# A fourth slot for attention features, and the second batch's statistics, gates and rotations moved ahead of the first scores

## Chip, cores and metric

The kernel runs on one core of one Trainium2 chip. The metric is the time of one execution on the device in microseconds (us), the median of several runs.

## The reference, cut to what matters

```python
x = L0_attn_x                                  # (8, 512, 128) fp32, 8 batches of 512 tokens
mod = (silu(c) @ wmod).reshape(8, 6, 1, 128)   # sa, ca, ga, sb, cb, gb; ga, gb kept at least 0.25 in size
h = layernorm(x) * (1 + ca) + sa
q, k, v = split(h @ qkv_w.T + qkv_b)           # 16 heads of 8
q, k = rope(q), rope(k)
attn = softmax(causal(q @ k.T / sqrt(8)))      # (8, 16, 512, 512)
x = x + ga * ((attn @ v) @ proj_w.T + proj_b)
h = layernorm(x) * (1 + cb) + sb
y = square(relu(h @ W_fc.T)) @ W_proj.T
x = x + gb * spikes(y) / 5                     # how often in 5 steps an integrator passes its threshold: 0 to 5
```

## The kernel before, in words

The work is cut into **halves**: half n is 8 of the 16 heads of batch n // 2, so there are 16 halves. Each engine runs a list of instructions in its own order, written out by hand, and the lists meet at semaphores. There is no scheduler.

Of each half the scores are made twice. First `scores_for_max` (L548, L554) makes them with queries in rows, in 21 banks called k, and VectorE takes the negated maximum of each row (`maxima`, L978). GpSimd splits the maxima in two bf16 parts, TensorE transposes them (L565 for the first half, L578), ScalarE copies them out (`mrow`, L833 and L841), and SyncE writes them by DMA into two extra rows of the query features `qf` (L429, L434), so that the second product subtracts them. Then `scores_for_exp` (L593, L598) makes the transposed scores in 18 banks called u, ScalarE takes exponentials (L827), and `probs_times_v` (L611) multiplies them with the values. The main loop counts slots u, 18 a half and 36 a batch; `at` is the slot within the batch. Maxima run ahead by up to 31 banks (`scores_ahead`): half 2b+2 is needed at about slot 9 of batch b, half 2b+3 at about slot 27.

The features of a head are its rotated queries and keys in three bf16 parts each (`parts` 0, 1, 2). After `rotary` on VectorE (L1014, `rot_c` and `rot_s`), the sum `whole` and what is left after a part (`rest`, L1299, and part 2, L1303) come from GpSimd, parts 0 and 1 from ScalarE (L885). SyncE stores every part to DRAM (`store_part`, L396) and reads them back spread over partitions: `spread_queries` (L409, 576 KB) and `spread_keys` (L420, three DMAs of 192 KB). They land in slot n % RING of `qf` and `kf`. `spread_queries(n)` waits until the slot's last user, half n - RING, has made its last transposed scores (`t_ready`). All DMAs are issued by SyncE, in its order.

Around this lie, one batch ahead, the layer norm (`statistics1`, `normalise1`, GpSimd's `deviation1`), its transposition (`a_task` T1), the products for queries (QK), keys (QK + 1) and values (V_); and one batch behind, the outputs' moves (`move_outputs`, L440 and L444), reciprocals of the sums (`reciprocals`, L1020, L448, L453), the normalised outputs `o_n` (L1325), and on TensorE the projection (PROJ, slot 16), then T2, FC and Y_ of the feed-forward part (`D_AT`, `Y_AT`), all in `d_bank`.

Ahead of the loop, TensorE does both batches' first tasks, mixed with `keep_warm`: products of a table with the identity that nobody reads. One call with SEQ columns is the same shape as a query or key task. Then come 22 banks of the first scores, each with a filler of 160 columns.

```python
def spread_queries(n, own=slice(0, HH), done=None):
    ...
    reach(sp, t_ready, NU * (n - RING + 1))
```

## Time and profile before

| | us |
|---|---|
| median of 3 runs | 441.04 |
| lowest and highest run | 440.73, 445.44 |
| the profiled execution's own time | 443.15 |
| its span in the trace | 441.4 |
| TensorE's matmuls busy | 390.9 (89% of the span) |
| VectorE busy | 329.3 (75%) |
| ScalarE busy | 256.8 (58%) |
| GpSimd busy | 126.1 (29%) |

The span is the time between the first and the last instruction of the trace. The execution's own time has 1.75 us around it. That execution was 2.1 us above the median. A busy engine is not the same as a bound: where an engine is waited for is read from the waits.

### The profile page before, as it was taken

To read this page: it belongs to the slowest core of one execution; us is meant where nothing else is said; L and a number is where in the kernel's file an instruction comes from. 1 tells how busy PE (TensorE), PEld (TensorE's weight loads), DVE (VectorE), ACT (ScalarE), POOL (GpSimd) and SP (SyncE) were. 2 spreads that over 40 slices of the span, in tenths; PEclk is the share of its full clock that TensorE was granted. 3 is DMA by queue.
4 is the path that set the end of the run, shared out by engine and by line. 5 is a ranking of instruction groups with operands and counts; after the bars stand their busy time and mean duration, and the time that the engine had idled before them with its cause. 6 is when DMAs were issued, how large, how long until landed. Compare 5 with 4: busy or idle time off the path is not lost.

```text
span 441.4 us, 15622 instructions
## 1 busy us (share of the span) xinstructions
PE 390.9 (89%) x6599; PEld 253.1 (57%) x6599; DVE 329.3 (75%) x730; ACT 256.8 (58%) x447; POOL 126.1 (29%) x163
## 2 busy tenths in 40 slices
PE   2778899888999989998899999998998889988885
PEld 2327555555656755666457654765566646753653
DVE  6659995886886988878986997699866777541176
ACT  8203465565676756765666665766665457566523
POOL 6714310430343043503342234304330220040020
PEclk9989999999999999999999999999999899998999
DMA  7056363243314233242415251323233050011001
GB/s 214 22 161 169 99 218 88 70 116 102 104 45 119 75 101 93 80 122 49 137 50 139 64 138 48 117 72 99 67 113 86 16 146 6 25 45 27 3 1 49
DMA packets 26050, 38.53 MB, mean 87 GB/s; under 512 B 5796, under 2 KB 20716, under 8 KB 23692
## 3 DMA queue, kind: packets, MB, share of 16 engines
q1 hardware_dynamic: 25980, 37.53, 29.8%
q8 instruction: 52, 0.85, 0.8%
q14 instruction: 18, 0.15, 0.1%
HBM read 26.35 MB, written 8.65 MB: 79 GB/s over the span
## 4 chain that ended last, share of the span: by engine, by line
PE 41%; DMA 18%; DVE 13%; ACT 10%; POOL 6%; issue 5%; SPq 5%; ACTq 0%; POOLq 0%; DVEq 0%
PE o_bank L611 10%; DMA kf<-k_scr 9%; PE d_bank L528 7%; DVE negmax L978 6%; PE t_bank L593 6%; PE s_bank L548 5%; DMA rden<-r_scr 4%; ACT probs L827 4%; PE a_bank L528 3%; DMA r_scr<-rden_c 2%; POOL parts L1303 2%; PE s_bank L528 2%; SPq L440 2%; PE t_bank L528 2%; POOL o_n L1325 2%
## 5 line engine op out<-in xcount | busy, mean ns | idle before, releaser
L978 DVE TENSOR_REDUCE negmax<-s_bank 128x1 f32<-128x512 f32 (+7 forms) x368 | 192.9, 566 | 56.9 <-PE s_bank L554 54.6
L827 ACT ACTIVATE probs<-t_bank 128x512 f32<-128x512 f32 x288 | 163.0, 594 | 89.8 <-PE t_bank L598 84.5
L548 PE MATMUL s_bank<-kf,qf 126*64 126x512 bf16 (+7 forms) x1024 | 118.7, 293 | 11.8 <-DMA kf<-k_scr 6.2
L593 PE MATMUL t_bank<-qf,kf 128*64 128x512 bf16 (+7 forms) x1024 | 113.3, 290 | 10.8 <-ACT probs L827 9.8
L611 PE MATMUL o_bank<-probs,v 128*32 128x512 f32 (+7 forms) x1024 | 75.1, 412 | 0.0
L548 PEld LDWEIGHTS s_bank<-kf,qf 126*64 126x64 bf16 x1024 | 50.6, 111 | 40.6 <-DVE negmax L978 19.9
L554 PE MATMUL s_bank<-causal,identb 128*64 128x64 bf16 x1024 | 72.6, 195 | 0.0
L598 PE MATMUL t_bank<-causal_t,identb 128*64 128x64 bf16 x1024 | 64.8, 195 | 0.0
L593 PEld LDWEIGHTS t_bank<-qf,kf 128*64 128x64 bf16 x1024 | 41.4, 110 | 35.1 <-ACT probs L827 14.4
L598 PEld LDWEIGHTS t_bank<-causal_t,identb 128*64 128x64 bf16 x1024 | 48.1, 111 | 9.3 <-issue 0.2
L554 PEld LDWEIGHTS s_bank<-causal,identb 128*64 128x64 bf16 x1024 | 47.1, 112 | 8.3 <-issue 8.1
L611 PEld LDWEIGHTS o_bank<-probs,v 128*32 128x32 f32 x1024 | 26.8, 109 | 36.3 <-issue 23.4
L1293 POOL TENSOR_TENSOR whole<-rot_c,rot_s 128x512 f32<-128x512 f32 x15 | 19.1, 1274 | 53.9 <-DVE rot_s L1014 53.9
L528 PE MATMUL d_bank<-wpr_sb,sq 128*64 128x128 f32 x448 | 30.1, 276 | 0.0
L1271 POOL CAST mparts<-negmax 128x32 bf16<-128x32 f32 x15 | 3.2, 211 | 94.2 <-DVE negmax L978 94.2
L528 PEld LDWEIGHTS d_bank<-wpr_sb,sq 128*64 128x64 f32 x448 | 24.0, 137 | 4.2 <-issue 3.0
L1303 POOL TENSOR_TENSOR parts<-rest,parts 128x512 bf16<-128x512 f32 x15 | 17.5, 1169 | 30.0 <-ACT parts L885 30.0
L528 PE MATMUL d_bank<-h2T,wfc_sb 128*64 128x512 f32 x96 | 25.5, 609 | 0.0
L1325 POOL TENSOR_TENSOR o_n<-o_t,rden 128x512 f32<-128x512 f32 x7 | 9.5, 1360 | 47.6 <-DMA rden<-r_scr 47.6
L1014 DVE SCALAR_TENSOR_TENSOR rot_c<-a_bank,bqk_sb,cos_sb 128x512 f32<-128x512 f32 x14 | 10.5, 750 | 16.3 <-PE a_bank L528 15.7
L528 PE MATMUL t_bank<-cos_sb,ident 128*64 128x160 f32 (+2 forms) x152 | 22.6, 404 | 0.0
L885 ACT CAST parts<-whole 128x512 bf16<-128x512 f32 x15 | 9.3, 618 | 22.4 <-POOL whole L1293 22.3
(145 smaller groups left out, 455.9 us busy)
## 6 DMA issues: line engine op xcount, KB each, us to landing
qf<-q_scr SPq DMA_DIRECT2D x15, 576.0 KB
kf<-k_scr SPq DMA_DIRECT2D x45, 192.0 KB
q_scr<-parts SPq DMA_DIRECT2D x24, 128.0 KB, 1.7
k_scr<-parts SPq DMA_DIRECT2D x24, 128.0 KB, 1.7
xa<-in_x SPq DMA_DIRECT2D x8, 256.0 KB, 3.9
o_t<-o_raw SPq DMA_DIRECT2D x60, 32.0 KB, 2.4
rden<-r_scr SPq DMA_DIRECT2D x15, 128.0 KB
out_y<-count SPq DMA_DIRECT2D x7, 256.0 KB, 6.7
```

The costliest lines, as they stand in the source:

```text
L528: last = nc.tensor.matmul(bank[own, cols], weights[:, own], data, start=start, stop=stop)
L548: nc.tensor.matmul(bank[C * a:C * (a + 1), col:col + keys], qf[0:KS, slot, 2 * p + a, C * i:C * (i + 1)], kf[0:KS, slot, 2 * p + a, 0:keys ...
L554: last = nc.tensor.matmul(bank[C * a:C * (a + 1), end - C:end], identb[:, C * a:C * (a + 1)], causal[:, C * a:C * (a + 1)], start=False, s ...
L593: nc.tensor.matmul(bank[C * a:C * (a + 1), col:col + w], kf[0:KX, slot, 2 * p + a, C * kb:C * (kb + 1)], qf[0:KX, slot, 2 * p + a, C * kb: ...
L598: last = nc.tensor.matmul(bank[C * a:C * (a + 1), col:col + C], identb[:, C * a:C * (a + 1)], causal_t[:, C * a:C * (a + 1)], start=False, ...
L611: last = nc.tensor.matmul(o_bank[32 * p:32 * (p + 1), C * kb:SEQ], v32[:, b % 2, NP * kb + HP * half + p, :], probs[:, v, col:col + w], st ...
L827: nc.scalar.activation(probs[:, v, :], t_bank[u % 2][:, :], ACT.Exp, scale=SCALE).then_inc(e_done, 1)
L978: last = nc.vector.tensor_reduce(own[:, i, p:p + len(same)], cols, AX.X, ALU.max, negate=True)
L1014: nc.vector.scalar_tensor_tensor(dst[to, qk, :], bank[of, :], bqk_sb[of, qk:qk + 1], table[of, :], ALU.add, ALU.mult).then_inc(rotated if ...
L1293: nc.gpsimd.tensor_tensor(whole[:, qk, :], rot_c[:, qk, :], rot_s[:, qk, :], ALU.add)\
L1303: nc.gpsimd.tensor_tensor(parts[:, qk, 2, :], rest[:, qk, :], parts[:, qk, 1, :], ALU.subtract).then_inc(split_done, 1)
L1325: nc.gpsimd.tensor_tensor(o_n[:, :], o_t[:, :], rden[:, :], ALU.mult).then_inc(on_done, 1)
```

## The change

It does six things.

- `RING` goes from 3 to 4 slots of features. The memory comes from sharing: `rest` is `rot_s`, `sq` is `relu` (squares are made in place), the modulation weights lie in `relu`, the row of ones in `count`. `rotary` waits for the last batch's split where it writes `rot_s`.
- SyncE issues the queries of half 2b+4 at the end of batch b, one store ahead of its keys' last part; the keys keep their place.
- The projection goes from slot 16 to 17, the residual from 18 to 19, the second reciprocals from slot 10 to 9.
- VectorE does the second batch's statistics, the gates' sizes and the normalisation ahead of the first rotation, and both rotations of the second batch ahead of the first maxima.
- TensorE does the second batch's values ahead of the first scores, and two long fillers there in place of four ahead of the second batch's transposition.
- ScalarE clears the fourth slot between steps of the start. GpSimd writes the ones beside the values by partition halves, with no `affine_select`. All parts of the second batch are stored ahead of the first maxima's rows.

```diff
--- before.py
+++ after.py
@@ -34,7 +34,7 @@
 NP = H // 2
-RING = 3
+RING = 4
 HALF = SEQ // 2
@@ -87,7 +87,7 @@
 
-D_AT = {16: PROJ, 25: T2, 27: FC, 29: FC + 1, 31: FC + 2, 33: FC + 3}
+D_AT = {17: PROJ, 25: T2, 27: FC, 29: FC + 1, 31: FC + 2, 33: FC + 3}
 Y_AT = {36: 0, 37: 1, 38: 2, 39: 3}
@@ -179,14 +179,12 @@
         ct_sb = sb("ct_sb", [P, NB])
-        wmod_sb = sb("wmod_sb", [P, 6 * P])
         cos_sb = sb("cos_sb", [P, SEQ])
...
         causal_t = sb("causal_t", [P, P], BF16)
-        ones_row = sb("ones_row", [MR, SEQ], BF16)
         minus_half = sb("minus_half", [P, NT])
@@ -210,7 +208,8 @@
         whole = sb("whole", [P, 2, SEQ])
-        rest = sb("rest", [P, 2, SEQ])
+
+        rest = rot_s
         parts = sb("parts", [P, 2, NPART, SEQ], BF16)
@@ -239,8 +238,13 @@
         relu = sb("relu", [P, NF, SEQ])
-        sq = sb("sq", [P, NF, SEQ])
+
+        sq = relu
+
+        wmod_sb = relu[:, 0:2, :].rearrange("p i c -> p (i c)")[:, 0:6 * P]
         count = sb("count", [P, 2, SEQ])
+
+        ones_row = count[0:MR, 0, 0:SEQ // 2].bitcast(BF16)
 
@@ -464,26 +468,24 @@
             sp.wait_ge(ones_made, 1)
-            sp.wait_ge(zeros_made[2], 2)
+            for slot in (2, 3):
+                sp.wait_ge(zeros_made[slot], 2)
             sp.dma_start(kf[KS:KX].rearrange("r s h c -> r (s h) c"),
...
             sp.dma_start(g_scr, gate_t[:, :]).then_inc(gates_stored, 16)
-            for j in range(NPART):
-                store_part(1, 0, j)
+            for qk in range(2):
+                for j in range(NPART):
+                    store_part(1, qk, j)
             place_first_maxima(0)
-            spread_queries(2)
-            for j in range(NPART):
-                store_part(1, 1, j)
-            spread_keys(2)
+            spread(2)
             place_first_maxima(1)
...
                     store_part(b + 1, 1, 2)
-                if 0 < b < final:
-                    spread(2 * b + 2)
+                    spread_keys(2 * b + 2)
                 if b == 0:
@@ -511,6 +513,7 @@
                     store_part(b + 2, 1, 1)
+                    spread_queries(2 * b + 4)
             spread_reciprocals(final, 0)
@@ -711,17 +714,16 @@
             pe.wait_ge(rotary_loaded, 16 * 2)
-            keep_warm(t_bank[1], SEQ, 4)
             a_task(1, T1)
...
             a_task(1, QK + 1)
+            a_task(1, V_)
+            keep_warm(t_bank[1], SEQ, 2)
             for k in range(NS_FIRST + 3):
...
                 keep_warm(t_bank[1], 160)
-                if k == 5:
-                    a_task(1, V_)
             transpose_first_maxima(0)
@@ -850,7 +852,7 @@
                 if b == 0:
-                    act.wait_ge(v_placed_ones, 1)
+                    act.wait_ge(v_placed_ones, 2)
                 for a in range(2):
@@ -898,18 +900,20 @@
             modulate1(0)
-            for j in range(2):
-                take_part(0, 0, j)
+            take_part(0, 0, 0)
             place_values(0)
+            take_part(0, 0, 1)
             modulate1(1)
+            clear(3, qf)
             act.wait_ge(d_ready, SETUP_TASKS)
             nc.scalar.copy(gate_t[:, :], d_bank[0:3 * NB, 0:P]).then_inc(gates_out, 1)
+            clear(3, kf)
             take_part(1, 0, 0)
...
             take_part(1, 0, 1)
-            first_maxima_out(0)
             for j in range(2):
                 take_part(1, 1, j)
+            first_maxima_out(0)
 
@@ -1007,7 +1011,7 @@
                 dve.wait_ge(a_ready, 4 * b + QK + qk + 1)
-                reach(dve, whole_done, 2 * (b - 1) + qk + 1)
+                reach(dve, whole_done if step == 0 else split_done, 2 * (b - 1) + qk + 1)
                 to, of, dst, table = ((slice(0, P), slice(0, P), rot_c, cos_sb),
@@ -1074,7 +1078,7 @@
 
-            def gates():
+            def gate_sizes():
                 for n, j in enumerate((2, 5)):
@@ -1087,6 +1091,8 @@
                 last.then_inc(mod_step, 1)
+
+            def gates():
                 dve.wait_ge(d_ready, 2)
@@ -1124,6 +1130,10 @@
             normalise1(0)
+
+            statistics1(1)
+            gate_sizes()
+            normalise1(1)
             dve.wait_ge(wqk_loaded, 16 * 2)
@@ -1131,16 +1141,12 @@
             first_k_parts()
-            statistics1(1)
-            normalise1(1)
             gates()
...
                 rotary(1, 0, step)
-            for k in range(NS_FIRST):
-                maxima(k)
             for step in range(3):
                 rotary(1, 1, step, bank=d_bank)
-            for k in range(NS_FIRST, scores_ahead(-1)):
+            for k in range(scores_ahead(-1)):
                 maxima(k)
@@ -1161,9 +1167,9 @@
                 if b > 0:
-                    if at == (8 if b == final else 10):
+                    if at == (8 if b == final else 9):
                         reciprocals(b - 1, 1)
-                    if at == 18:
+                    if at == (18 if b == final else 19):
                         residual1(b - 1)
@@ -1348,22 +1354,20 @@
             for a in range(2):
-                ones = v32[:, :, :, 16 + HD * a:16 + HD * (a + 1)].rearrange("p k g d -> p (k g) d")
-                nc.gpsimd.memset(ones, 1.0).then_inc(v_cleared, 1)
-                pool.wait_ge(v_cleared, 2 + a)
-                last = nc.gpsimd.affine_select(out=ones, in_=ones, pattern=[[0, 2 * NC * NP], [0, HD]], fill=0.0,
-                                               compare_op=ALU.is_ge, base=(C - 1, -C)[a],
-                                               channel_multiplier=(-1, 1)[a])
-            last.then_inc(v_placed_ones, 1)
+                ones = v32[C * a:C * (a + 1), :, :, 16 + HD * a:16 + HD * (a + 1)].rearrange("p k g d -> p (k g) d")
+                nc.gpsimd.memset(ones, 1.0).then_inc(v_placed_ones, 1)
+
+                pool.wait_ge(v_placed_ones, a + 1)
+            deviation1(1)
             rotary_sum(0, 0)
...
             left(0, 0, 2)
-            deviation1(1)
             for qk in range(2):
...
                 left(1, qk, 2)
-                split_first_maxima(qk)
+            for pairs in range(2):
+                split_first_maxima(pairs)
 
```

VectorE near the program's start, around the first batch's rotations (`st`, `mv` are statistics, `xn` the normalised input, `sign` and `big` the gates' sizes). Before:
```order
L994 TENSOR_SCALAR xn<-xa,mv,rs 128x128 x4
L1014 SCALAR_TENSOR_TENSOR rot_c<-a_bank,bqk_sb,cos_sb 128x512
L1014 SCALAR_TENSOR_TENSOR rot_s<-a_bank,bqk_sb,sin_sb 64x512 x2
L1014 SCALAR_TENSOR_TENSOR rot_c<-d_bank,bqk_sb,cos_sb 128x512
L1014 SCALAR_TENSOR_TENSOR rot_s<-d_bank,bqk_sb,sin_sb 64x512 x2
L1101 TENSOR_TENSOR whole<-rot_c,rot_s 128x512
L1105 CAST parts<-whole 128x512
L1108 TENSOR_TENSOR rest<-whole,parts 128x512
L1112 CAST parts<-rest 128x512
L1115 TENSOR_TENSOR parts<-rest,parts 128x512
L983 BN_STATS st<-xa 128x6 x4
L989 BN_AGGR mv<-st 128x2 x4
```
In the change:
```order
L1079 TENSOR_SCALAR mod<-mod 128x8 x2
L998 TENSOR_SCALAR xn<-xa,mv,rs 128x128 x4
L987 BN_STATS st<-xa 128x6 x4
L993 BN_AGGR mv<-st 128x2 x4
L1083 TENSOR_SCALAR sign<-mod 128x8
L1084 SCALAR_TENSOR_TENSOR big<-mod 128x8
L1083 TENSOR_SCALAR sign<-mod 128x8
L1084 SCALAR_TENSOR_TENSOR big<-mod 128x8
L1088 TENSOR_SCALAR big<-big 128x16
L1091 SCALAR_TENSOR_TENSOR gate<-sign,big 128x8 x2
L998 TENSOR_SCALAR xn<-xa,mv,rs 128x128 x4
L1018 SCALAR_TENSOR_TENSOR rot_c<-a_bank,bqk_sb,cos_sb 128x512
```
The second batch's statistics, gate sizes and normalisation, which stood behind the first key parts, now stand ahead of the first rotation.

SyncE at the end of batch 0 and the start of batch 1 (`kf`, `qf` are the features' slots, `k_scr` the keys' parts in DRAM). Before:
```order
L396 DMA k_scr<-parts 128x512
L434 DMA qf<-mrow 2x4x1024
L448 DMA r_scr<-rden_c 64x64
L396 DMA k_scr<-parts 128x512 x2
L409 DMA qf<-q_scr 72x1x4096
L420 DMA kf<-k_scr 24x1x4096 x3
L453 DMA rden<-r_scr 64x1x512
```
In the change:
```order
L400 DMA k_scr<-parts 128x512
L438 DMA qf<-mrow 2x4x1024
L452 DMA r_scr<-rden_c 64x64
L400 DMA k_scr<-parts 128x512
L413 DMA qf<-q_scr 72x1x4096
L400 DMA k_scr<-parts 128x512
L424 DMA kf<-k_scr 24x1x4096 x3
L457 DMA rden<-r_scr 64x1x512
```
The queries' load went ahead of the last store of a key part; the keys' loads stayed behind it.

TensorE around the projection of batch 0, in batch 1 (`wo_g`, `o_n`: gated projection weights and normalised outputs). Before:
```order
L593 MATMUL t_bank<-qf,kf 64x256 x4
L598 MATMUL t_bank<-causal_t,identb 64x64 x4
L528 MATMUL d_bank<-wo_g,o_n 64x128 x8
L548 MATMUL s_bank<-kf,qf 64x192 x4
L548 MATMUL s_bank<-kf,qf 64x64 x4
L554 MATMUL s_bank<-causal,identb 64x64 x8
L593 MATMUL t_bank<-qf,kf 64x256 x4
L598 MATMUL t_bank<-causal_t,identb 64x64 x4
L548 MATMUL s_bank<-kf,qf 64x128 x8
```
In the change:
```order
L596 MATMUL t_bank<-qf,kf 64x256 x4
L601 MATMUL t_bank<-causal_t,identb 64x64 x4
L551 MATMUL s_bank<-kf,qf 64x192 x4
L551 MATMUL s_bank<-kf,qf 64x64 x4
L557 MATMUL s_bank<-causal,identb 64x64 x8
L596 MATMUL t_bank<-qf,kf 64x256 x4
L601 MATMUL t_bank<-causal_t,identb 64x64 x4
L531 MATMUL d_bank<-wo_g,o_n 64x128 x8
L551 MATMUL s_bank<-kf,qf 64x128 x8
```
One slot's scores (192 and 64 columns of one kind, 256 of the other) went ahead of the projection.

## Rows read from the trace of the kernel before

**Rows 1.** Busy time by stretch: PE, PEld, DVE, ACT, POOL; granted clock, DMA share, GB/s.
```profile
45.00:58.00 13.00, 10.96 (x210) 7.45 (x208) 12.97 (x35) 5.41 (x10) 3.96 (x6) 1.00 0.44 123
...
123.00:170.00 47.00, 44.57 (x814) 29.33 (x810) 39.48 (x88) 30.52 (x55) 14.73 (x18) 1.00 0.34 94
```
**Rows 2.** What TensorE's matmuls waited for: total us, times, longest.
```profile
PE t_bank L593 <- ACT probs L827: 9.8, 21, 1.2
PE s_bank L548 <- DMA kf<-k_scr: 6.2, 6, 1.4
...
PE d_bank L528 <- POOL o_n L1325: 5.7, 5, 1.5
```
**Rows 3.** Timeline of VectorE's start: start us, us, instruction, idle before it.
```profile
14.69 0.75 DVE L1014 SCALAR_TENSOR_TENSOR rot_c<-a_bank,bqk_sb,cos_sb 128x512 f32<-128x512 f32 x1 [4.38 <-PE a_bank L528]
...
23.91 0.86 DVE L983 BATCH_NORM_STATS2 st<-xa 128x6 f32<-128x128 f32 x4
...
34.05 3.28 DVE L978 TENSOR_REDUCE negmax<-s_bank 128x1 f32<-128x512 f32 x6
37.75 3.06 DVE L978 TENSOR_REDUCE negmax<-s_bank 128x1 f32<-128x320 f32 x6 [0.43 <-PE s_bank L554]
...
40.73 0.74 DVE L1014 SCALAR_TENSOR_TENSOR rot_c<-d_bank,bqk_sb,cos_sb 128x512 f32<-128x512 f32 x1
41.50 1.53 DVE L1014 SCALAR_TENSOR_TENSOR rot_s<-d_bank,bqk_sb,sin_sb 64x512 f32<-64x512 f32 x2
```
**Rows 4.** Timeline of TensorE's start.
```profile
17.15 1.97 PE L644 MATMUL a_bank<-wv_sb,hT 128*64 128x64 f32 x32 [0.91 <-DVE rot_s L1014]
...
27.96 1.08 PE L624 MATMUL a_bank<-ident,xn 128*128 128x128 f32 x4 [2.16 <-DVE xn L994]
...
32.20 1.08 PE L528 MATMUL d_bank<-hT,wqk_sb 128*64 128x512 f32 x4 [0.34 <-ACT gate_t L906]
33.11 0.39 PE L548 MATMUL s_bank<-kf,qf 126*64 126x512 bf16 x2
```
**Rows 5.** Timeline, SyncE, first feature loads.
```profile
25.71 2.06 SPq L420 DMA_DIRECT2D kf<-k_scr  x3
```
**Rows 6.** Busy time of two stretches at the lower clock, columns as Rows 1.
```profile
27.90:31.20 3.30, 3.24 (x12) 1.30 (x12) 0.93 (x8) 0.78 (x1) 0.00 (x0) 0.50 0.53 163
...
348.90:352.10 3.20, 3.20 (x57) 3.20 (x55) 1.01 (x3) 0.42 (x1) 0.62 (x1) 0.50 0.02 5
```
**Rows 7.** Timeline of TensorE, waits on feature loads.
```profile
218.46 0.41 PE L548 MATMUL s_bank<-kf,qf 126*64 126x512 bf16 x2 [1.20 <-DMA kf<-k_scr]
...
338.59 0.41 PE L548 MATMUL s_bank<-kf,qf 126*64 126x512 bf16 x2 [1.31 <-DMA kf<-k_scr]
```
**Rows 8.** Timeline of SyncE, loads of halves 2b+2 and 2b+3.
```profile
138.19 0.87 SPq L409 DMA_DIRECT2D qf<-q_scr  x1
139.46 2.10 SPq L420 DMA_DIRECT2D kf<-k_scr  x3
...
203.18 0.69 SPq L434 DMA_DIRECT2D qf<-mrow  x1
207.51 0.83 SPq L409 DMA_DIRECT2D qf<-q_scr  x1
...
326.70 0.87 SPq L409 DMA_DIRECT2D qf<-q_scr  x1
```
**Rows 9.** Chain that ended last, SyncE's loads of half 4.
```profile
93.03 3.41 DMA k_scr<-parts
```
**Rows 10.** Timeline, outputs' moves on SyncE and the projection on TensorE.
```profile
145.01 2.68 SPq L440 DMA_DIRECT2D den<-o_raw  x4
...
158.74 1.09 PE L528 MATMUL d_bank<-wo_g,o_n 128*64 128x128 f32 x16 [1.53 <-POOL o_n L1325]
...
160.28 0.22 PE L548 MATMUL s_bank<-kf,qf 126*64 126x128 bf16 x1
...
348.55 1.86 PE L528 MATMUL d_bank<-wo_g,o_n 128*64 128x128 f32 x16 [1.53 <-POOL o_n L1325]
```

## The prediction

> **What bounds the kernel now.** I read three views in this order: busy time by stretch, what TensorE waited for, and the timelines of the places the change touches. In a steady batch TensorE is busy 44.6 of 47 us and VectorE 39.5 [rows 1]. So TensorE sets the pace, and each of its waits is lost time. Its matmuls waited 6.2 us, 6 times, for loads of features, 5.7 us, 5 times, for normalised outputs ahead of the projection, and 9.8 us in 21 short waits for exponentials [rows 2]. The start is different: from 45 to 58 us VectorE is busy 12.97 of 13 us and TensorE 10.96 [rows 1]. From the first maximum at 34.05 VectorE runs without idle time, but for 0.43 us, into this stretch [rows 3]. There each microsecond taken off VectorE, or by which the first scores start sooner, brings the loop forward.
>
> The profiled execution took 443.15 us, 2.1 above the median of 441.04. The sum is made against the former; what of it the median run lacks is said below.
>
> **The start.** Before, the second batch's statistics ran at 23.91 behind the first key parts [rows 3], so its transposition started at 27.96 after 2.16 us of idle TensorE [rows 4]. VectorE had been idle for 4.38 us ahead of 14.69 [rows 3]. The moved work fits in there: 0.86 for the statistics, and I estimate 3.5 in all with aggregation, gate sizes, GpSimd's deviation and the normalisation (the same chain ran from 23.91 to before 27.96). If it overruns, the first rotation is some 0.2 late. The transposition then follows the first values, which ScalarE places by about 20.5, so it runs 7 us sooner. The queries' product follows at 22.6. VectorE finishes the key parts at 24 as before and rotates the second batch's queries to 27.4 (three instructions, 0.74 + 1.53 = 2.3 us, as at 40.73 and 41.50 [rows 3]); the keys' product and rotation follow.
>
> Before its first score TensorE now has the values, which need that first rotation done: 27.4, then 1.97 at the lower clock of 1.2 GHz [rows 4] or half of that at 2.4. Then come two fillers, each of the shape of the keys' product. That took 1.08 [rows 4], or 0.9 from start to start; at the lower clock both fillers take 3.4, at the higher 1.7. So the first score stands at 30.2 (all at 2.4 GHz) to 32.9 (all at 1.2), against 33.11 [rows 4]. Before, the granted clock was 0.50 from 27.9 to 31.2, behind the idle time ahead of 27.96 [rows 6]. Now TensorE has short rests in the same place, so I expect part of the work at the lower clock. The load of the first heads' keys is issued by 27.77 [rows 5] in both kernels and landed somewhere before 33.1, which no row pins down. I take 31.6: 1.5 us gained, with bounds 0 and 2.9.
>
> On top of that the second batch's key rotation leaves the run of maxima: 2.3 us (40.73 to 43.05). The stall of 0.43 at 37.75, when TensorE had the values between two scores, goes too [rows 3]. That is 2.8. The extra queue entries are covered: ScalarE's two clearings lie in waits for the gates and the first rotations, GpSimd loses two selections, and SyncE's single store of ones follows loads that end at the same time. The second batch's six part stores now precede the first row of maxima, but the parts are ready by about 37 (two chains of some 5.5 us behind rotations that end at 27.4 and 30), while the first half's first maxima end at about 39. Start in all: **4.3** (2.8 to 5.7; if TensorE and not VectorE sets the pace, about 2).
>
> **The fourth slot, odd halves.** Half 2b+3 was loaded only when half 2b had made its last transposed scores: in batch 3 SyncE had placed the maxima at 203.18 and stood until 207.51 [rows 8]. Now the load follows the maxima at once, 3.6 us sooner. The waits there were 0.8, 1.2 (at 218.46 [rows 7]) and 1.3, all under 3.6. All go: **3.3**.
>
> **The fourth slot, even halves.** The other three waits (1.4, 0.2, and 1.3 at 338.59 [rows 7]) are on half 2b+2. Here the slot was not what held the load. The keys wait for the store of their last part, and that stays: keys were issued 1.3 us behind the queries' issue [rows 8]. Only the queries move, ahead of that store, about 1.3 us sooner. The load as a whole took 11.9 us from 326.70 to the wait's end at 338.6 [rows 7, 8]. If it is the amount of data that takes this time, 1.3 us come off the end. Against it stands that the last part's small store now meets 576 KB of queries. In one batch the trace shows such a meeting, with the queries issued 0.4 us behind the store: the store took 3.41 us [rows 9], where others let the keys go 1.3 us after the queries. I expect the keys issued 2 us later and faster, since the queries are then through. The net lies between all 2.9 us gained and, at 2 us in each of six halves, 9 lost. I take **1.0**, because the total data are the same and begin sooner.
>
> The rule that speaks against this move is in the Trainium skill, DMA: Bandwidth & Descriptors, section Queues, rings and completion order: on each engine a queue's descriptors are consumed in ring order, so a small store behind a large load waits for it. The 3.41 us point the same way. Taken strictly it gives the first rival below.
>
> **The projection one slot later.** TensorE waited 1.53 us twice for `o_n` before the projection at the higher clock (one at 158.74), again 1.53 at 348.55, and less in two batches that had waited for features first [rows 10]. The chain from the outputs' moves at 145.01 to the projection at 158.74 is made of SyncE's issues and three DMAs, and no edit shortens it by much: the reciprocals come a slot sooner, but SyncE is still issuing the moves when they are ready. The slot put ahead of the projection is short: the projection ends at 159.8 and slot 18's scores start at 160.28 [rows 10], so 0.5 to 0.6 us. So each wait shrinks by 0.6 and does not go, and where a wait for features goes ahead of it, it grows. Of 5.7 us I take **2.0** off (0 to 4.4).
>
> **The clock.** Behind the wait at 348.55 the granted clock was 0.50 (1.2 GHz) for 3.2 us, and the projection took 1.86 where 1.09 is usual [rows 6, 10]. That cost some 1.4 us. I give it only to the profiled execution, which was 2.1 above the median.
>
> The tiles that now share memory cost nothing: the rotations wait for a split that was done a batch ago, and squares in place have the same shape. The reciprocal in slot 9 may meet sums that have not landed, with maxima queued behind it; the chain gives it at most a slot, VectorE has 7.5 us of slack a batch, and I take **-0.5** in all.
>
> Sum: 4.3 + 3.3 + 1.0 + 2.0 - 0.5 = 10.1. With the clock's 1.4 the profiled execution would have come to 443.15 - 11.5 = 431.6; the median goes from 441.04 to 430.9. I predict **431**.
>
> **Rivals.**
> 1. The last key part stands behind the queries, and even halves wait longer. For: the 3.41 us. Against: the data start sooner. At 1 us each in six halves that is 6 where 2.9 were: 1.0 turns to -3.1, and the time to 435. At 2 us each it is -9.1, and 441.
> 2. No gain from an earlier first score, through the lower clock in the fillers or the load's landing: 2.8 or less of the 4.3, so 432.4 to 434. For: the clock fell in this place before.
> 3. Better than forecast: first score at 30.2 (+1.4), no waits on even halves (+1.9), a chain of outputs that is shorter because less traffic meets it (+2.4): 441.0 - 10.1 - 5.7 = 425.2.
> 4. Slower than before: rival 1, decided when the keys land more than about 2 us behind their slot. TensorE then stands 3 us six times and drops to 1.2 GHz each time, as at 348.9, for 1.4 more: 26.4 less the 2.9 of before is 23.5 lost against 9.1 won elsewhere, so 455. Only a store that takes 7 us instead of 3.4 would do it, which no row shows.
>
> **Chances.** Forecast (428.5 to 432.5) 0.52; rival 2 (432.4 to 434) 0.15; rival 1 at 1 to 2 us (433.5 to 441) 0.16; rival 3 (424 to 428.5) 0.13; rival 4 0.04. A change of 1%, 4.4 us, is about what a measurement of this kernel can tell from none. Faster than 436.6 is the forecast, rivals 2 and 3 and half of rival 1: 0.88. Within 1%: 0.08. Slower: 0.04. The range leaves out the better half of rival 3 and the worse half of 1 and 4: 425.5 to 436.5.
>
> **What would show it.** First score near 31.6 and the 22nd maximum near 44.5, against 48.9; no wait for `kf` around slot 27; queries issued ahead of the last key store, whose landing takes 3 to 4 us; waits for `o_n` of 0.5 to 1 us; a steady batch of some 46 us. A start of the first transposed scores no sooner than 46 would refute the start's term, waits on `kf` above 1 us in even halves that of the fourth slot.

## The result and the profile after

The changed kernel takes 443.00 us in the median of 20 runs (439.83 to 446.66), the kernel before 440.46 (435.67 to 447.50). The ratio is 1.0076, with a 95% interval of 1.0052 to 1.0100: slower by 0.8%, where 431 was forecast. The profiled execution took 444.07 with a span of 442.3. Ratios and intervals leave out executions more than 1.5% above the quickest of their kernel, medians don't, so a ratio is not the quotient of the two medians, least of all in experiments 4, 6, 7 and 8, where 17 of 31 executions of the kernel before are left out.

What TensorE's matmuls waited for, total us, times and longest, against [rows 2]:

```profile
PE s_bank L551 <- DMA kf<-k_scr: 15.1, 7, 4.4
...
PE d_bank L531 <- POOL o_n L1331: 0.9, 1, 0.9
```

The waits for features were to fall from 6.2 us and rose to 15.1. One of the seven, 2.4 us, is at the start. The other six, 12.7 us, all stand ahead of even halves (2.9 before). On odd halves there is none, as forecast. The wait for outputs is down to 0.9 us, once. SyncE's queue shows why. Its timeline around the load of half 4 in batch 1, against [rows 8]:

```profile
135.82 0.69 SPq L438 DMA_DIRECT2D qf<-mrow  x1
...
137.78 0.86 SPq L413 DMA_DIRECT2D qf<-q_scr  x1
138.73 0.46 SPq L400 DMA_DIRECT2D k_scr<-parts  x1
143.90 2.11 SPq L424 DMA_DIRECT2D kf<-k_scr  x3
```

Before, the keys' load went out 1.3 us behind the queries' [rows 8]. Now SyncE stands from 139.2 to 143.9, because the keys' load waits for the small store at 138.73, and that store waits behind 576 KB of queries. In each of the six batches the store is seen landed 6.1 to 7.3 us after the queries' issue. The DMA engines are busy until 1 to 2 us before that, so the large load is by all signs through by then as well. In this batch, by stretch (columns as rows 1, the last but one is the DMA engines' busy share):

```profile
141.00:142.00 1.00, 1.00 (x21) 0.87 (x18) 0.00 (x0) 0.00 (x0) 0.00 (x0) 1.00 0.85 221
142.00:143.00 1.00, 1.00 (x18) 0.39 (x14) 0.69 (x1) 0.04 (x1) 0.00 (x0) 1.00 0.58 171
143.00:144.00 1.00, 1.00 (x22) 0.93 (x20) 0.00 (x0) 0.97 (x2) 0.00 (x0) 1.00 0.08 26
```

In total SyncE waited so:

```profile
SPq L424 <- DMA k_scr<-parts: 31.6, 7, 5.9
```

It was 8.8 us in eight waits before. What is queued behind on SyncE is late as well, the sums of the outputs among it: VectorE waited 18.3 us for them in seven times, against 2.6 in one. The first of the six waits and that of batch 1 (timeline of TensorE):

```profile
102.11 0.64 PE L551 MATMUL s_bank<-kf,qf 126*64 126x512 bf16 x2 [4.42 <-DMA kf<-k_scr]
...
150.70 0.41 PE L551 MATMUL s_bank<-kf,qf 126*64 126x512 bf16 x2 [1.17 <-DMA kf<-k_scr]
```

Behind three of these six waits (4.42, 1.96 and 2.02 us) the clock falls, as it did in [rows 6]. Busy time by stretch (columns as rows 1):

```profile
98.00:101.00 3.00, 0.00 (x0) 0.00 (x0) 0.21 (x1) 0.40 (x1) 0.46 (x2) 0.87 0.49 147
101.00:104.00 3.00, 1.89 (x16) 0.90 (x20) 0.65 (x2) 0.56 (x1) 0.00 (x0) 0.50 0.32 77
104.00:107.00 3.00, 3.00 (x26) 0.95 (x20) 0.44 (x1) 0.04 (x1) 0.00 (x0) 0.50 0.04 8
```

TensorE did nothing from 98 to 101, then worked at a granted clock of 0.50 (1.2 GHz). The same happened at 199 and 343 (0.54, 0.50). Behind a wait of 2.24 us at 247 it did not (1.00 from 247 to 250). On the chain that ended last, one group of 24 products of probabilities and values took 3.57, 3.52 and 3.00 us in the three places, where 1.86 is usual:

```profile
89.01 6.12 DMA k_scr<-parts
...
96.59 5.48 DMA kf<-k_scr
102.11 0.64 PE s_bank L551 x2
103.34 3.57 PE o_bank L614 x24
...
124.75 1.86 PE o_bank L614 x24
...
138.73 5.15 DMA k_scr<-parts
...
148.82 3.08 DMA den<-o_raw
```

The chain shows a second way in which the late store costs time. At 102, 199 and 343 it runs through the keys' load. In the other three batches it leaves SyncE by the outputs' moves, which are queued behind the keys' load, and reaches TensorE through the sums (`den`) or the outputs scaled by them. Both ways start at the same store. No experiment tells their shares apart.

The start came out as forecast on VectorE, and less so on TensorE. The lines are VectorE's statistics that follow the maxima of the 22nd bank, before and after, then TensorE's first transposed score before, and its first scores and first transposed score after:

```profile
48.92 0.86 DVE L983 BATCH_NORM_STATS2 st<-xa 128x6 f32<-128x128 f32 x4
```

```profile
45.55 0.86 DVE L987 BATCH_NORM_STATS2 st<-xa 128x6 f32<-128x128 f32 x4
```

```profile
48.70 0.38 PE L593 MATMUL t_bank<-qf,kf 128*64 128x512 bf16 x2
```

```profile
32.40 0.41 PE L551 MATMUL s_bank<-kf,qf 126*64 126x512 bf16 x2 [2.37 <-DMA kf<-k_scr]
...
46.55 0.41 PE L596 MATMUL t_bank<-qf,kf 128*64 128x512 bf16 x2 [0.99 <-DMA qf<-mrow]
```

The first score waited 2.4 us for its keys, and the clock stayed full (1.00 from 28 to 34). The first transposed score came 2.2 us sooner than before and met a new wait, for the rows of maxima.

### The profile page after: what moved, and what is told of

Same layout as the page of the kernel before. It is cut to its first block, busy times and chain, and to the rows that moved or that the text cites. A ratio compares the mean times of both kernels' runs of the same rounds, so it can differ in the third digit from the quotient of the medians.

```text
span 442.3 us, 15605 instructions
## 1 busy us (share of the span) xinstructions
PE 389.0 (88%) x6591; PEld 251.2 (57%) x6591; DVE 328.8 (74%) x730; ACT 260.5 (59%) x449; POOL 121.8 (28%) x161
## 4 chain that ended last, share of the span: by engine, by line
PE 44%; DMA 16%; DVE 12%; ACT 10%; SPq 7%; POOL 5%; issue 4%; ACTq 0%; POOLq 0%; DVEq 0%
PE o_bank L614 12%; DMA k_scr<-parts 8%; PE s_bank L551 7%; PE t_bank L596 7%; DMA kf<-k_scr 5%; PE d_bank L531 5%; DVE negmax L982 5%; ACT probs L829 4%; PE a_bank L531 3%; SPq L424 3%; PE t_bank L531 2%; ACT parts L887 2%; PE t_bank L601 2%; SPq L444 1%; PE s_bank L557 1%
## 5 line engine op out<-in xcount | busy, mean ns | idle before, releaser
L551 PE MATMUL s_bank<-kf,qf 126*64 126x512 bf16 (+7 forms) x1024 | 118.4, 292 | 19.1 <-DMA kf<-k_scr 15.1
L596 PE MATMUL t_bank<-qf,kf 128*64 128x512 bf16 (+7 forms) x1024 | 112.9, 290 | 11.8 <-ACT probs L829 9.8
L614 PE MATMUL o_bank<-probs,v 128*32 128x512 f32 (+7 forms) x1024 | 79.7, 431 | 0.0
L551 PEld LDWEIGHTS s_bank<-kf,qf 126*64 126x64 bf16 x1024 | 49.5, 110 | 47.6 <-DVE negmax L982 17.5
L596 PEld LDWEIGHTS t_bank<-qf,kf 128*64 128x64 bf16 x1024 | 41.1, 111 | 35.7 <-ACT probs L829 13.7
L531 PE MATMUL d_bank<-wpr_sb,relu 128*64 128x128 f32 x448 | 30.1, 276 | 0.0
L531 PEld LDWEIGHTS d_bank<-wpr_sb,relu 128*64 128x64 f32 x448 | 24.0, 137 | 4.2 <-issue 3.0
L1309 POOL TENSOR_TENSOR parts<-rot_s,parts 128x512 bf16<-128x512 f32 x15 | 17.4, 1162 | 25.1 <-ACT parts L887 25.1
L1018 DVE SCALAR_TENSOR_TENSOR rot_s<-a_bank,bqk_sb,sin_sb 64x512 f32<-64x512 f32 x28 | 21.0, 750 | 0.9
L1024 DVE RECIPROCAL rden_c<-den 64x64 f32<-64x64 f32 x15 | 8.1, 540 | 18.3 <-DMA den<-o_raw 18.3
```

The lines of the kernel that those rows point to most:

```text
L531: last = nc.tensor.matmul(bank[own, cols], weights[:, own], data, start=start, stop=stop)
L551: nc.tensor.matmul(bank[C * a:C * (a + 1), col:col + keys], qf[0:KS, slot, 2 * p + a, C * i:C * (i + 1)], kf[0:KS, slot, 2 * p + a, 0:keys ...
L596: nc.tensor.matmul(bank[C * a:C * (a + 1), col:col + w], kf[0:KX, slot, 2 * p + a, C * kb:C * (kb + 1)], qf[0:KX, slot, 2 * p + a, C * kb: ...
L614: last = nc.tensor.matmul(o_bank[32 * p:32 * (p + 1), C * kb:SEQ], v32[:, b % 2, NP * kb + HP * half + p, :], probs[:, v, col:col + w], st ...
L1018: nc.vector.scalar_tensor_tensor(dst[to, qk, :], bank[of, :], bqk_sb[of, qk:qk + 1], table[of, :], ALU.add, ALU.mult).then_inc(rotated if ...
L1309: nc.gpsimd.tensor_tensor(parts[:, qk, 2, :], rest[:, qk, :], parts[:, qk, 1, :], ALU.subtract).then_inc(split_done, 1)
```

## Experiments

Each kernel is the changed one with the edit shown, if nothing else is said. Ratios are to the kernel before, measured beside it on the same chip. Its median was 442.15 beside experiments 1, 2, 3 and 5, and 441.83 beside 4, 6, 7 and 8, these eight all on one chip. It was 441.61 beside 9 to 12, on a second chip, and 439.49 beside 13 to 15, on a third.

**1. The queries back behind the keys' last store.**

```diff
                     store_part(b + 1, 1, 2)
-                    spread_keys(2 * b + 2)
+                    spread(2 * b + 2)
...
                     store_part(b + 2, 1, 1)
-                    spread_queries(2 * b + 4)
```

> The change with one edit undone: the queries of half 2b+4 are issued behind the last store of a key part again, as before, while the fourth slot stays. Theory A (the last key part's store waits behind 576 KB of queries, so keys are issued 5 us later): the store takes under 2 us again, the waits for kf on even halves fall from 12.7 to 3 us or less, no wait on odd halves, the clock stays at 2.4 GHz there, and the time is 431 to 434 us. Rival B (the second reciprocals in slot 9 make VectorE wait for den, 18.3 us in all, and that is the loss): the queries' place matters little and the time stays at 438 or more.

432.47 us, ratio 0.9824 (0.9769 to 0.9878). This one line moved costs 10.5 us. Rival B falls: the reciprocals still stand in slot 9, the time comes back all the same, and VectorE's wait for the sums falls from 18.3 to 6.6 us. SyncE's timeline in batch 1:

```profile
130.46 0.69 SPq L438 DMA_DIRECT2D qf<-mrow  x1
131.21 0.49 SPq L452 DMA_DIRECT2D r_scr<-rden_c  x1
131.94 1.56 SPq L400 DMA_DIRECT2D k_scr<-parts  x2
133.59 0.87 SPq L413 DMA_DIRECT2D qf<-q_scr  x1
134.86 2.10 SPq L424 DMA_DIRECT2D kf<-k_scr  x3
```

```profile
PE s_bank L550 <- DMA kf<-k_scr: 4.5, 4, 1.4
PE d_bank L530 <- POOL o_n L1330: 3.7, 5, 1.2
```

Measured from the issue of the maxima's row, which is the same point of the program, the keys' load goes out at +4.4 here and at +8.1 to +9.3 in the changed kernel. TensorE needs them at about +13.7 (150.70 - 1.17 - 135.82), in the first of the six batches at +11.7. Where it had to wait, the load had landed at +13.1 (first batch), +14.3 and +15.0 here. In the changed kernel it was +16.1 in the first batch and +14.6 to +16.0 in the others. The load of keys itself is shorter there (6.5 to 7.5 us against 8.7 to 10.6 here), since the queries are through by then. So of the delay of 3.7 to 4.7 us a part is won back. The waits on even halves are 12.7 us there and 3.3 here (1.4, 0.6 and 1.3), which makes 9.4. The wait at the start is 1.2 us longer there, and the three groups at 1.2 GHz cost 4.5. Waits for outputs, for maxima and for their rows are together 3.3 us shorter there. This adds up to 11.8 us, where the two spans differ by 11.1.

A single trace is only a sample of such waits. Experiment 15 is the same kernel again, and its trace has one wait for features, of 1.0 us, where this one has four with 4.5.

**2. The queries ahead, on ScalarE's queue.** ScalarE issues this load itself, behind the copy of the last key part but one:

```diff
+                act.wait_ge(t_ready, NU * (n - RING + 1))
+                act.dma_start(qf[0:FR, n % RING, :],
...
+                    if TAKE_AT[at - PER_BATCH] == (1, 1):
+                        spread_queries_act(2 * b + 4)
```

> The change, but the queries of half 2b+4 are issued by ScalarE, on its own DMA queue, at the same time as SyncE issued them. Theory A as order within one queue: the store no longer stands behind the queries, takes about 2 us, and the time is 431 to 434. Theory A2 (it is the load of the 16 DMA engines, whichever queue it came from): the store still takes 4 to 6 us, keys are as late as in the change, and the time stays at 440 or more. Four sixths of a microsecond of ScalarE a batch are hidden in its idle time.

433.39 us, ratio 0.9838 (0.9787 to 0.9889). ScalarE's queue, then SyncE's:

```profile
132.62 0.80 ACTq L899 DMA_DIRECT2D qf<-q_scr  x1
```

```profile
134.10 1.56 SPq L400 DMA_DIRECT2D k_scr<-parts  x2
139.21 2.19 SPq L424 DMA_DIRECT2D kf<-k_scr  x3
```

The store sits in another queue than the load and is slow all the same: SyncE's wait for it is 3.3 to 4.5 us, against 1.36 in experiment 1, where the store goes out just ahead of the queries. It lands 6.3 to 7.6 us after the queries' issue, about as in the changed kernel (6.1 to 7.3). So order within one queue isn't needed for the delay. What the two queues share is the 16 DMA engines, but no run shows these to be the reason. The outcome fits neither theory whole: the store is as slow as A2 has it, the time is A's. The queries leave 2 us sooner here (together with the maxima's row, not 2.0 us behind it), and so the keys go out at +6.3 to +7.6.

**3. The start alone.** Three slots, projection in slot 16, reciprocals in 10, loads as before; the new start. **4. The same with tiles of its own** in place of the shared ones.

> Only the start of the change, with the shared tiles: three slots, the loop's loads, projection, residual and reciprocals as before. If the start's gain of 3.4 us in the profile (VectorE reaches the 22nd maximum at 45.5 and not 48.9) is carried to the end: 437 us, with the waits of before on kf and o_n. If later waits take it up: 440.

> The start of the change alone, as in the run before (441.3 us), but with rest, sq, the modulation weights and the row of ones in tiles of their own again. If sharing tiles costs in the loop what the start gains: 438.5 to 439. If it costs nothing and the start's 3.4 us are lost elsewhere: 441 again.

441.31 and 441.59 us, ratios 1.0002 (0.9970 to 1.0033) and 1.0035 (0.9993 to 1.0077). The start by itself gives nothing that the timed runs show, and the shared tiles cost nothing that they show. In both cases the second reading was the right one.

**5. Experiment 1 with projection in 16, residual in 18 and reciprocals in 10.** So the fourth slot alone is added to experiment 3. **6. Experiment 1 with the projection in slot 18.**

> As e1, and the projection back in slot 16, the residual in 18, the second reciprocals in 10. So it is the fourth slot and the start, without the two moves of steps. If the moves are worth what the slot put ahead is (0.6 us in each of five batches), it is 2 to 3 us slower than e1; if they are worth nothing, within 1 us.

> The fastest so far (queries behind the last store, 432.5 us) with the projection in slot 18, the residual in 20 and its statistics in 21. It had 3.7 us of waits for o_n left. If slot 18 hides them and nothing behind the projection is late: 429.5 to 431. If the feed-forward part's next steps now wait (the transposition in slot 25 for the normalised residual): no gain, 432 to 434.

435.94 us, ratio 0.9894 (0.9843 to 0.9945), with 8.0 us of waits for outputs in five times; and 436.48, ratio 0.9918 (0.9871 to 0.9965). Beside experiment 3 the fourth slot brings 1.1% or 4.8 us. Projection and reciprocals together bring 0.7%, or 3.1 us, of experiment 1 against 5, with intervals that just overlap. Experiment 5 is 3.5 us slower than 1 by the medians, where 2 to 3 were forecast. In slot 18 the kernel took more than either reading had: no wait for outputs is listed, and waits of TensorE for maxima grow to 8.7 us from 2.9.

**7. Queries ahead of the last two key stores.** **8. Half of them ahead, half behind** (four heads each).

> The change, with the queries of half 2b+4 issued by SyncE ahead of both last stores of key parts (1.2 us sooner than in the change), which is about when ScalarE issued them in the run on its own queue (433.4 us). Theory Q (order within SyncE's queue holds the store): two stores now stand behind the queries, so it is as slow as the change or slower, 443 us or more. Theory L (the load on the DMA engines holds the store for a fixed time after the queries' issue, and that run was better for its earlier issue): keys go out about 1 us sooner than in the change and the time is 434 to 439.

> The change with only four of eight heads' queries (288 KB) ahead of the last store, the other four behind it. If the amount of data ahead sets the store's delay, it falls from 5.2 us to about 3, the waits for kf on even halves from 12.7 us to about 6, and the time is 436 to 440. If any load ahead costs the same, it stays at 442 or more.

439.38 us, ratio 0.9999 (0.9955 to 1.0042), and 434.37, ratio 0.9896 (0.9832 to 0.9959). The waits for features, of experiment 7 and of 8:

```profile
PE s_bank L551 <- DMA kf<-k_scr: 11.9, 6, 4.8
```

```profile
PE s_bank L555 <- DMA kf<-k_scr: 4.8, 3, 3.2
```

Experiment 7 fits neither theory. The keys went out only about 0.2 us sooner than in the change, so Theory L's microsecond didn't come, and 439.38 lies below Theory Q's 443. Experiment 8 came out better than its 436 to 440. With 288 KB ahead the keys go out 4.2 to 5.9 us after the first queries' issue, against 6.1 to 7.3 with 576 KB. So the delay grows with the amount of data ahead of the store.

With the issue of the keys' load, again from the maxima's row, in the six batches:

| queries | keys' load issued | waits for features in the loop, us | us |
|---|---|---|---|
| behind the store (1) | +4.4 to 4.8 | 3.3 | 432.47 |
| ahead, ScalarE's queue (2) | +6.3 to 7.6 | 3.4 | 433.39 |
| half ahead (8) | +6.1 to 7.9 | 4.8 | 434.37 |
| ahead of two stores (7) | +7.9 to 9.1 | 11.9 | 439.38 |
| ahead of one store (the change) | +8.1 to 9.3 | 12.7 | 443.00 |

Keys issued at +6 to +8 cost 1 to 2 us, and keys at +8 to +9 cost 7 to 10.5. Of the 3.6 us between the last two rows, which hardly differ in issue and waits, the table explains little.

**9. Experiment 1 with the old start.**

> The first experiment's kernel (fourth slot, queries behind the keys' last store, projection and reciprocals one slot later and sooner) with the start of the kernel before put back whole: order of VectorE, TensorE, GpSimd, stores and fillers as before, only the fourth slot's clearing added. The first experiment took 432.47. If the start is worth the 3.4 us by which its 22nd maximum came sooner, this one takes 435.5 to 436.5. If the start is worth nothing, as the two runs of the start alone had it, it stays at 432 to 433.5, and the fourth slot, the projection and the reciprocals carry the whole gain of 9 to 10 us against the kernel before.

435.07 us, ratio 0.9867 (0.9813 to 0.9922). By the ratios the start, together with the rest, is worth 0.4 to 0.5%, or 2 us, between the two readings. The intervals overlap, so this is not clear of noise. Its trace against that of experiment 1, the statistics that end VectorE's first run and the first transposed score:

```profile
48.20 0.87 DVE L989 BATCH_NORM_STATS2 st<-xa 128x6 f32<-128x128 f32 x4
```

```profile
47.99 0.38 PE L597 MATMUL t_bank<-qf,kf 128*64 128x512 bf16 x2
```

In experiment 1:

```profile
44.36 0.86 DVE L986 BATCH_NORM_STATS2 st<-xa 128x6 f32<-128x128 f32 x4
```

```profile
46.40 0.41 PE L595 MATMUL t_bank<-qf,kf 128*64 128x512 bf16 x2 [2.03 <-DMA qf<-mrow]
```

VectorE gains 3.8 us; TensorE gains 1.6, because the rows of maxima come 2.0 us late for it.

**10. The kernel before once more.**

> The kernel before itself, a second profiled execution. It asks how far the groups of waits vary between two executions of one kernel. If waits for the outputs and the features repeat within some 1.5 us (5.7 and 6.2 us) and the 22nd maximum ends within 0.5 us of 48.92, the differences read between the kernels' profiles stand. If they differ by 3 us or more, then a single profile can't carry the 3.4 us of the start or the 2 us of the outputs, and only the timed runs can.

A single run, 443.06 us. Waits for features 7.8 us, for outputs 7.2 (6.2 and 5.7 in the first profile). Its statistics behind the 22nd bank stood at 47.82 and not at 48.92, its first transposed score at 47.61 and not at 48.70, and its clock was full from 28 to 34. So 1.1 us of the start's difference lay in the profiled execution. These groups of waits repeat to 1.6 us, but between experiments 1 and 15 they differ by 3.5.

**11. Experiment 1 without the two long fillers. 12. Experiment 1 with the reciprocals in slot 10. 13. Both.**

```diff
             a_task(1, V_)
-            keep_warm(t_bank[1], SEQ, 2)
...
-                    if at == (8 if b == final else 9):
+                    if at == (8 if b == final else 10):
```

> The first experiment's kernel without the two long fillers (1.9 us) ahead of the first scores. The first score there waited 1.2 us for features, so it can come sooner by nothing: the fillers stood in a wait. If they do nothing but fill, the time stays within 1 us of 432.47. If they hold TensorE's clock up for the first scores, the granted clock falls to 0.50 around 31 us and the first 22 banks come later by 1 to 2 us, so 433.5 to 434.5.

> The first experiment's kernel with the second reciprocals in slot 10 again, the projection staying in 17. With projection and reciprocals both moved back it took 435.94 against 432.47, with 8.0 us of waits for the outputs. If the projection's slot carries this difference, the time is 432 to 433.5 and the waits for the outputs stay near 3.7 us. If the sooner reciprocals carry it, it is 434.5 to 436, with outputs' waits of 6 to 8 us; then VectorE's wait for the sums (6.6 us in five times) falls to the 2.6 of the kernel before.

> The first experiment's kernel without the two long fillers and with the second reciprocals in slot 10: the two edits that each came out below it, together. If they are worth what they showed apart (4.2 and 1.6 us), 426.5 to 428.5. If the fillers' part was the scatter between chips and calls, 430 to 431.5, as with the reciprocals alone.

428.31 us, ratio 0.9696 (0.9648 to 0.9745); 430.91, ratio 0.9760 (0.9719 to 0.9802); 429.27, ratio 0.9759 (0.9715 to 0.9804). Experiments 11 and 12 came out below what either reading had, and 13 between its two.

**14. The changed kernel without the long fillers. 15. Experiment 1 again, beside 13 and 14.**

> The changed kernel as it is, with the queries ahead of the keys' last store, without its two long fillers. If the queries ahead of the store carry the loss, they do it here too: waits for features of 12 to 15 us in all, the keys issued 8 to 9 us behind the maxima, and a time of 438.5 to 443. If the fillers were the larger part of the loss, the time falls below 435.

> The first experiment's kernel, measured beside the two kernels that differ from it and from the changed kernel by one edit each. It asks whether 432.47 holds next to them. If the fillers cost 4 us, it lies 3 to 5 us over the kernel without fillers and with reciprocals in slot 10 (and some 1.5 of these are the reciprocals'). If it comes out at 428 to 430, the fillers cost nothing and the difference was one between chips.

439.98 us, ratio 1.0001 (0.9974 to 1.0027), as the first reading has it, with 11.0 us of waits for features, and 431.98, ratio 0.9813 (0.9777 to 0.9848). The queries' place costs 3.1% without the fillers (14 against 11) and 2.5% with them. On the third chip alone it is 2.4% (14 against 13, which also has the reciprocals in 10), with intervals far apart. So it carries the loss. The repeat bears out experiment 1; it lies 2.7 us over 13, where 3 to 5 was one reading.

What the fillers cost is not settled. The ratios give 0.7% in the changed kernel (14), 1.2% in experiment 1 (11 against 1 or 15), and nothing beside 12 (13), but each of these pairs was measured on different chips. On one chip, experiment 12 (fillers in, reciprocals in 10) is 0.6% over 11 (fillers out, reciprocals in 9). On another, 15 (fillers in, reciprocals in 9) is 0.5% over 13 (fillers out, reciprocals in 10). If the two effects add up, this gives an estimate of 0.6% for the fillers and nothing for the reciprocals. The intervals overlap in both pairs. If there is a cost, it does not arise where they stand. Without them the first score still waited for its keys, and in experiment 11 the clock fell (in 14 it did not):

```profile
30.18 0.41 PE L550 MATMUL s_bank<-kf,qf 126*64 126x512 bf16 x2 [1.87 <-DMA kf<-k_scr]
...
46.92 0.41 PE L595 MATMUL t_bank<-qf,kf 128*64 128x512 bf16 x2 [1.94 <-DMA qf<-mrow]
```

```profile
31.00:34.00 3.00, 3.00 (x34) 2.23 (x32) 2.46 (x5) 0.45 (x2) 2.38 (x2) 0.60 0.62 187
```

The first transposed score is no sooner than in experiment 1 (46.40). From the first projection (108.2) to the start of the last one in `d_bank` (378.7) this trace takes 270.5 us, that of experiment 1 275.2 (107.9 to 383.1). But the trace of experiment 15, the same kernel as 1, takes 272.4, so more than half of that difference lies between two executions of one kernel. The best kernels are 11, 12 and 13: 2.4 to 3.0% faster than before.

## Why the prediction was wrong

**The step that failed** is "The fourth slot, even halves": "I expect the keys issued 2 us later and faster, since the queries are then through", and "I take **1.0**". The sign of the net is what failed: the store's delay was put at 2 us. From the maxima's row the keys went out 3.0 to 4.8 us later than before. They were faster indeed (6.5 to 7.5 us, 7.0 to 10.6 before), but not by as much. In the three batches where TensorE waited in both kernels they landed 3.0, 2.1 and 0.7 us later. The waits on even halves went from 2.9 to 12.7 us. Instead of 1.0 won, 9.8 were lost. That is what the text itself gave as the lower bound ("at 2 us in each of six halves, 9 lost", 441). The three groups of products at 1.2 GHz add 4.5 us (1.7, 1.7 and 1.1 over 1.86) in the profiled execution. Experiments 1, 7, 8 and 14 show the queries' place to be the cause; experiment 1 takes back 10.5 us. How much goes through TensorE's wait for keys, and how much through the outputs' moves behind it on SyncE, is open.

**Why the value was taken wrongly.** The 3.41 us [rows 9] were read as a sample of a store behind the load. That store was issued 0.4 us *before* the load. And it was so in all six batches of the trace before, which in the other five let the keys go 1.3 us after the queries. The chain that ended last in the kernel before has such a store in the sixth batch, seen landed 1.67 us after its issue:

```profile
326.28 1.67 DMA k_scr<-parts
```

So 3.41 us is not even the price of that meeting. It came again in the second execution of the kernel before (3.60), in the same batch, and not in experiment 1, where the order is the same; what held the store there is open. For a store behind the load no row existed. The load in progress is the bound there: the store was seen landed 6.1 to 7.3 us after the queries' issue, 1 to 2 us after the DMA engines had fallen nearly idle. Rival 4's "Only a store that takes 7 us instead of 3.4 would do it, which no row shows" had the mechanism, and 0.04 of the chance. It had the clock fall in all six halves, where it fell in three. The rule of the Trainium skill, DMA: Bandwidth & Descriptors, section Queues, rings and completion order, that a queue's descriptors are consumed in order on each engine, gave the right sign, and the trace after agrees (6.1 to 7.3 us). Experiment 2 shows that two queues don't spare the store, so order in one queue is not all of the reason.

**The start: 4.3 forecast, 0 to 2.2 measured.** VectorE gained 3.4 us. The sum counted VectorE's gain as TensorE's. What was late next, the rows of maxima on their way through GpSimd, TensorE, ScalarE and SyncE, took back 1.0 us in the changed kernel and 2.0 in experiment 1. And 1.1 us lay in the first profile, whose clock was at 0.50 from 28 to 31 where it was full in experiment 10. The bound "about 2", if TensorE sets the pace, was right. The first score was held by its keys, at 32.4 and not 31.6. Why the start alone (experiments 3 and 4) shows nothing at all in timed runs, while experiment 9 puts it at 2 us, stays open. The interval of experiment 3 and the overlap in 9 leave room for about 1 us in both.

**The fourth slot, odd halves: 3.3 forecast.** No wait is left on them. Experiment 5 against 3 gives 4.8 us for the slot with the old order of loads, and the waits on odd halves, 3.9 us in the trace of experiment 3, are gone in that of 5.

**Projection 2.0, reciprocals -0.5: together 1.5 forecast, 3.1 measured** (experiment 1 against 5). Waits for outputs fell from 5.7 to 3.7 us, as the step says, and in experiment 5 they were 8.0. The projection's slot carries this. Experiment 12 against 5 differs in it and the residual alone: 1.3% or 5.9 us, with intervals apart but on different chips, and waits for outputs of 3.0 against 8.0. So the projection's 2.0 was too small, and at 3 to 6 us perhaps outside its bounds of 0 to 4.4. The reciprocals in slot 9 bring nothing that the runs show: 430.91 without that move against 431.98 and 432.47 with it, with intervals that overlap. VectorE's wait for the sums was 6.6 us in experiment 1, 4.9 in 15, and 2.6 before.

Without the even halves' 1.0, the prediction's sum is 9.1, and 431.9 us. Experiment 1, which lacks only that edit, took 432.47 and 431.98. The agreement is luck in part: the start, taken too high, and the other terms, too low, made up for each other.

## What to carry to other kernels

A large load moved ahead of a small store that the next load waits for does not use idle time: the store landed only when the DMA engines were nearly idle again, with the load in either of the two queues. Measure such a move from a fixed point of the program to the moment at which the last piece lands, not to the moment at which the first is issued. A row is a bound for an order only if it has that order, with the store behind the load and not ahead of it; where none has it, take the load's whole duration as the bad end. And a gain on the engine that leads in a stretch counts only up to the next late thing, which was here a chain of four short steps.

## What was not expected

- A store of 128 KB issued just ahead of the 576 KB load is seen landed 1.4 us after the end of its issue, and one issued just behind it after 4.7 to 5.9 us, with the load in the same queue. With the load in ScalarE's queue it is 3.3 to 4.5 us. Both of the latter end 6 to 7.6 us after the load's issue.
- The first keys' load was issued at 25.77 or 25.78 us in the changed kernel and in experiments 11, 13 and 14, and the first score found it landed at 32.40, 30.18, 31.63 and 30.23. So a chain that hangs on one early load can differ by 2 us between executions whose programs are the same up to that load.
- Eight matmuls that nobody reads, in a wait at the start, bought nothing, although without them the clock fell behind that wait (0.60 from 31 to 34 in experiment 11). They may cost some 0.6%, which is not settled.
